# Graph attention layer with routed experts on one core: the last 29 additions of the edge loop in two halves of 132 columns, and the softmax steps of the last chunk in other slots

## What is computed

```
x = x + gnn(layernorm(x), edge_index, edge_attr)
  q = x@Wq+bq; k = x@Wk+bk; v = x@Wv+bv; e = edge_attr@We
  alpha = einsum(q[dst], k[src] + e) / sqrt(32)        # per edge and head
  ea    = exp(alpha - segment_max(alpha, dst)[dst])
  out   = segment_sum((v[src]+e) * ea/denom[dst], dst) + x@Ws+bs
x = x + ffn(layernorm(x))                               # top 2 of 8 experts, 256 -> 512 -> 256
```

## Time and profile before

| what | value |
|---|---|
| median of 3 runs | 2534.5 us (2531.59 to 2537.31) |
| profiled execution, its own time | 2541.5 us |
| span of its trace | 2539.7 us |
| edge loop, last score (L1047) starts | 1944.42 us |
| first addition of the drain starts, last one ends | 1945.44 and 1973.77 us |
| busy over the span: PE, DVE, ACT, POOL | 94, 80, 63, 72% |

### The profile page before, as it was taken

How to read it: one execution, slowest core, us unless ns; L and a number is a source line. 1 busy time by engine, 2 the same in 40 slices (tenths; PEclk the granted TensorE clock), 3 DMA queues, 4 the chain that set the end, 5 groups by cost and what they waited for, 6 DMA issues and landing times. The chain is left out here.

```text
span 2539.7 us, 67202 instructions
## 1 busy us (share of the span) xinstructions
PE 2381.0 (94%) x13310; PEld 1992.7 (78%) x13311; DVE 2021.1 (80%) x5247; ACT 1603.5 (63%) x4423; POOL 1829.9 (72%) x2194
## 2 busy tenths in 40 slices
PE   6998999999999999999999999999998657999998
PEld 3445788888888888888888888888886647999998
DVE  6865999999999999999999999999998863222222
ACT  1222677777677677767767777776776535666665
POOL 4213788888888888888888888887887704666666
PEclk9999999999999999999999999999999558999999
DMA  7325787777777777777777877777777652434443
GB/s 233 130 107 183 235 227 223 225 228 228 219 226 228 222 226 228 222 219 226 227 219 225 230 222 226 226 227 213 228 224 215 196 157 50 71 63 64 69 66 53
DMA packets 337646, 476.68 MB, mean 188 GB/s; under 512 B 61270, under 2 KB 268444, under 8 KB 337004
## 3 DMA queue, kind: packets, MB, share of 16 engines
q0 software_dynamic: 92576, 259.72, 38.2%
q1 hardware_dynamic: 238444, 213.23, 28.6%
q10 hardware_dynamic: 6288, 0.05, 0.1%
HBM read 425.40 MB, written 50.57 MB: 187 GB/s over the span
## 5 line engine op out<-in xcount | busy, mean ns | idle before, releaser
L824 POOL DMA_INDIRECT kv_ring<-vk_table,tab_c x880 | 860.1, 977 | 287.8 <-issue 179.9
L978 PE MATMUL ps_e<-we_sb,aT 128*128 128x256 f32 x3520 | 919.8, 384 | 29.7 <-DVE ve_ke L1065 24.3
L978 PEld LDWEIGHTS ps_e<-we_sb,aT 128*128 128x128 f32 x3520 | 600.9, 191 | 105.5 <-issue 51.3
L1059 DVE TENSOR_TENSOR ve_ke<-kv_ring,ps_e 128x512 f32<-128x512 f32 x880 | 601.0, 683 | 37.9 <-PE ps_e L982 16.2
L834 POOL TENSOR_TENSOR ve_ke<-ve_ke 128x256 f32<-128x256 f32 x880 | 552.7, 632 | 18.8 <-ACT factor L951 5.2
L1029 PE MATMUL ps_u<-ve_ke,sel 128*128 128x264 f32 x1760 | 545.6, 392 | 21.2 <-POOL ve_ke L834 7.0
L911 ACT COPY aT<-ps_t 128x256 f32<-128x256 f32 x880 | 325.8, 370 | 308.2 <-PE ps_t L966 278.0
L982 PE MATMUL ps_e<-q_slots,selT 128*128 x1760 | 517.8, 375 | 0.0
L1129 DVE SCALAR_TENSOR_TENSOR node_slots<-node_slots,same_tile,ps_u 128x264 f32 x880 | 423.9, 482 | 28.2 <-PE ps_u L1029 21.2
L982 PEld LDWEIGHTS ps_e<-q_slots,selT 128*128 128x128 f32 x1760 | 335.2, 190 | 45.9
L1047 DVE TENSOR_REDUCE alpha<-ve_ke 128x8 f32<-128x256 f32 x880 | 366.4, 416 | 5.4 <-issue 3.4
(11 more groups left out here) (251 smaller groups left out, 2687.9 us busy)
## 6 DMA issues: line engine op xcount, KB each, us to landing
a_ring<-in_edge_attr SPq DMA_DIRECT2D x880, 128.0 KB
loc_c<-loc_table SPq DMA_DIRECT2D x220, 128.0 KB
kv_ring<-vk_table,tab_c POOLq DMA_INDIRECT x880
vk_table<-kv_out SPq DMA_DIRECT2D x49, 256.0 KB, 2.0
skip_table<-skip_out SPq DMA_DIRECT2D x49, 128.0 KB, 1.7
out<-node_slots SPq DMA_DIRECT2D x1, 6144.0 KB
node_slots<-skip_table SPq DMA_DIRECT2D x2, 2688.0 KB, 16.8
w_sb<-in_L_ffn_W SPq DMA_DIRECT2D x2, 2048.0 KB, 9.5
```

The costliest lines, as they stand in the source:

```text
L824: g.indirect_dma_start(out=kv_ring[:, i % N_KV, :], out_offset=None, in_=vk_table, in_offset=bass.IndirectOffsetOnAxis(ap=tab_c[:, c % N_T ...
L978: t.matmul(ps_e[i % 2][:, 0:D], aT[i % 2][:, k * P:(k + 1) * P], we_sb[:, k, :], start=(k == 0), stop=(k == KD - 1))
L1059: v.tensor_tensor(ve_ke[:, to:ke + 1:ke - to, 0:D], kv.rearrange("p (t d) -> p t d", t=2), e[:, None, :].to_broadcast([P, 2, D]), ALU.add) ...
```

## The change

Three things are changed, all after the last score.

- In `emit(NCH, ...)` and `emit(NCH + 1, ...)`, that is for all 29 additions of the drain, VectorE adds columns 0 to 131 and columns 132 to 263 in an instruction each. The first half waits for a new semaphore `first_half_added` of the item before (the first of all for `acc_added`), the second half for `acc_added`, which only second halves count.
- The softmax parts of the last chunk stand in other slots: VectorE 2, 3, 4, 5, 6 instead of 3, 4, 6, 7, 8; TensorE 0, 2, 4, 6 instead of 0, 3, 6, 10; ScalarE 1, 2, 6 instead of 3, 4, 11.
- GpSimd applies the mask of the last chunk in slot 11 instead of 5, so behind eleven weighed items (its products) instead of five.

```diff
-            s, at, grant = counters(c3, a_turned=N_A, aT_ready=2, e_ready=2, ve_added=N_KV, kq_ready=2,
+            s, at, grant = counters(c3, a_turned=N_A, aT_ready=2, e_ready=2, ve_added=N_KV, first_half_added=0, kq_ready=2,
...
-            def over_chunks(eng, emit, **kw):
+            def over_chunks(eng, emit, last_parts={}, **kw):
...
-                emit(NCH, NCH % 2, plan(scores=False, **kw))
+                emit(NCH, NCH % 2, plan(scores=False, **dict(kw, parts=last_parts)))
...
-                over_chunks(pool, emit, what="weigh", parts={5: "mask"})
+                over_chunks(pool, emit, what="weigh", parts={5: "mask"}, last_parts={11: "mask"})
...
-                over_chunks(act, emit, what="select", parts={3: "apart", 4: "offs", 11: "exp"})
+                over_chunks(act, emit, what="select", parts={3: "apart", 4: "offs", 11: "exp"},
+                            last_parts={1: "apart", 2: "offs", 6: "exp"})
...
-                over_chunks(pe, emit, what="sum", parts={0: "keys", 3: "scores", 6: "minima", 10: "turn_scores"})
+                over_chunks(pe, emit, what="sum", parts={0: "keys", 3: "scores", 6: "minima", 10: "turn_scores"},
+                            last_parts={0: "keys", 2: "scores", 4: "minima", 6: "turn_scores"})
...
-                def add(c, i, n, before):
+                IN_HALVES_FROM = (NCH - 2) * CH + CH - LAG["add"]
+
+                def add(c, i, n, before, in_halves):
                     m = c * CH + i
                     to, sofar = [sums_flat[:, bass.ds(k * SLOT, UW)] for k in (n, before)]
                     dve.wait_ge(s["summed"], at("summed", m))
+                    if in_halves:
+                        split = m - IN_HALVES_FROM
+                        half = UW // 2
+                        if split:
+                            dve.wait_ge(s["first_half_added"], split)
+                        else:
+                            dve.wait_ge(s["acc_added"], at("acc_added", m - 1))
+                        v.scalar_tensor_tensor(out=to[:, 0:half], in0=sofar[:, 0:half], scalar=same_tile[:, m:m + 1], in1=ps_u[i % 2][:, 0:half],
+                                               op0=ALU.mult, op1=ALU.add).then_inc(s["first_half_added"], 1)
+                        dve.wait_ge(s["acc_added"], at("acc_added", m - 1))
+                        v.scalar_tensor_tensor(out=to[:, half:UW], in0=sofar[:, half:UW], scalar=same_tile[:, m:m + 1], in1=ps_u[i % 2][:, half:UW],
+                                               op0=ALU.mult, op1=ALU.add).then_inc(s["acc_added"], 1)
+                        return
...
-                            add(c - back, i, n, before)
+                            add(c - back, i, n, before, c >= NCH)
...
-                over_chunks(dve, emit, what="add", parts={3: "scan", 4: "scan_back", 6: "own", 7: "least", 8: "shift"})
+                over_chunks(dve, emit, what="add", parts={3: "scan", 4: "scan_back", 6: "own", 7: "least", 8: "shift"},
+                            last_parts={2: "scan", 3: "scan_back", 4: "own", 5: "least", 6: "shift"})
```

## The result

The changed kernel takes 2544.5 us, the median of 6 runs (2542.83 to 2548.24), against 2533.2 us for the kernel before in the same rounds (2531.39 to 2537.31): a ratio of 1.0045, 95% interval 1.0032 to 1.0058, so 8.1 to 14.7 us slower. The forecast was 2539.2 in a range of 2532 to 2545. The direction was right, and the time lies half a microsecond inside the upper end of the range, but the cost is 11.3 us by the medians, 2.4 times the 4.7 us of the sum.

What follows compares the result with a forecast made beforehand. The prediction took VectorE's sequencer work per addition to bound the drain. Halves 3.9, last item 0.1 and softmax steps 0.7 sum to +4.7 us on 2534.5, giving 2539.2 us, range 2532 to 2545.

Steps and rivals of the forecast that it cites:

- VectorE's sequencer is the bound: Drain additions: the sequencer's work per item sets their distance, which goes from 0.83 to 0.97 us, +3.9 us; chance 0.70.
- The third case: Drain additions: data are the bound, 0.69 us per item with halves, -3.1 us in all, 2531.4 us; chance 0.10.
- the second (the sequencer waits for the engine): Drain: next load only once the engine has taken the second half, 0.27 us per item, 2542.9 us; chance 0.10.
- The load behind least: Drain, item 8: by a skill rule this table load would run ahead, item 8 and the sum 0.6 us less.
- The fourth case: Drain: TensorE, granted half its clock throughout, becomes the bound at 1.06 us per item, 2541.7 us; chance 0.10.
- The softmax steps: Drain, items 3 to 15: stalls of 3.5 us against 2.8 with the new slots, +0.7 us, bounds -0.3 and +1.3.
- The hole behind least: Drain, items 8 to 9: the sum of item 9 waits behind turn_scores, so its addition comes 1.88 us after item 8.
- The mask costs nothing: GpSimd, last chunk: the mask waits for the last alpha until 1945.02 anyway and no drain sum needs a product; 0 us.
- nothing outside these 28 us is changed: Whole kernel: the change touches only the drain of 28.33 us, from first to last halved addition; no cost elsewhere.
- Everything up to 1945 as before: Sign expected in the new profile: all rows ahead of the drain's additions unchanged, 0 us.
- what the drain gains or loses should pass to the end one for one: Drain's end: later stages start from a barrier after the last addition, so all +4.7 us reach the total.
- worth nothing, and nothing waits for it later: ScalarE's exponential in the drain: about 1.5 us earlier, but its weights are first needed after 1958; gain 0.

## Why the prediction was right, and where it was not

**Right: VectorE's sequencer is the bound, and each item gets 0.14 us dearer.** The distance went from 0.83 to 0.97 in every kernel with halves. Without the table load and its register work it fell to 0.68 and 0.74. The third case (the data) wanted 0.69 with the loads in place, the second (the sequencer waits for the engine) 1.10; both are out. The load behind least did not run ahead of it: least starts at 1951.11, the load at 1951.1, and item 8 comes 1.74 us behind item 7, as forecast (1.72).

**The fourth case, TensorE at half its clock, came in part.** It was priced for the whole drain. For TensorE alone (us, busy, granted clock, DMA share, GB/s), four stretches of the drain of the changed kernel:

```profile
1944.20:1948.30 4.10, 3.98 (x11) 0.50 1.09 371
1952.60:1958.90 6.30, 6.07 (x13) 0.50 0.98 318
1959.10:1965.80 6.70, 3.60 (x11) 1.00 0.00 1
1966.10:1969.00 2.90, 2.90 (x6) 0.50 0.00 0
```

Between and behind the three stretches at 0.50 the clock is at or near 1.00. By the mean clocks of the drain, 0.79 and 0.94, some 14 us of 34.89 run at the 1.2 GHz level, against some 3.5 of 28.33 in before (an estimate). Two of the additions of the last such stretch, VectorE in order of time:

```profile
1967.25 0.35 DVE L1139 SCALAR_TENSOR_TENSOR node_slots<-node_slots,same_tile,ps_u 128x132 f32 x1 [0.55 <-PE ps_u L1030]
...
1969.37 0.35 DVE L1139 SCALAR_TENSOR_TENSOR node_slots<-node_slots,same_tile,ps_u 128x132 f32 x1 [0.54 <-PE ps_u L1030]
```

The additions ahead start at 1966.09 and 1968.22, so 1.16 and 1.15 us earlier instead of 0.97, and TensorE ends the wait. The distances are 1.16, 0.97, 1.15 and 0.97 in turn, 1.06 in the mean, just the chain that the prediction gave for half the clock. Behind item 9 there are two more of 1.15 and 1.14. The four together cost 0.7 us. Why the clock falls where it does stays open: it fell behind pauses of TensorE of 3.44, 2.39 and 1.65 us here, and did not fall in before behind one of 1.93 (ahead of the sum at 1961.47).

**The softmax steps: right in kind, small in size.** The hole behind least was forecast at 1.88 us, the first halves show 1951.94 to 1954.31, 2.37. TensorE and VectorE in order of time, which answer to the earlier trace rows:

```profile
1952.47 0.28 DVE L1103 TENSOR_TENSOR least<-ps_ak,least 128x128 f32<-128x128 f32 x1
1954.31 0.35 DVE L1139 SCALAR_TENSOR_TENSOR node_slots<-node_slots,same_tile,ps_u 128x132 f32 x1 [1.56 <-PE ps_u L1030]
...
1952.81 0.47 PE L1024 MATMUL ps_rx<-ident,least 128*128 128x128 f32 x1 [2.39 <-DVE least L1103]
1953.08 6.21 PE L1030 MATMUL ps_u<-ve_ke,sel 128*128 128x264 f32 x12
```

The mechanism is the one described: turn_scores waits for shift, and the sum of item 9 stands behind it. But transpose and sum ran slow there, at a granted clock of 0.50 behind 2.39 us of idle TensorE: the upper bound of that term. Item 3 to item 15 takes 16.66 us in the changed kernel, 15.91 with the mask put back, 15.16 in the forecast; the rescaling in the drain takes 2.33 and 2.51 instead of 2.76, and the fifteen distances behind it 15.3 and 15.2 instead of 14.6, in the changed kernel by the two distances at half clock above and one pause of 0.35 us (below).

**Wrong: "The mask costs nothing."** This is the step that failed. It looked at what waits for a product or the mask and found nobody, which is true: with the factor in PSUM nothing ahead of T0 is late. What it did not look at is what GpSimd's products do to VectorE while they run. The prediction had eleven products back to back from 1937.55 to 1944.4, and the rescaling stood right in that stretch. This is also where "nothing outside these 28 us is changed" and the sentence on the change, "all after the last score", went wrong: the mask's slot is behind the last score in the program, but GpSimd's row of products starts 10.30 us ahead of T0 in time. "Everything up to 1945 as before" was the sign that would have shown it, and it did not hold. The row cost 3.41 us ahead of T0 and 0.5 to 0.7 behind it. The second part goes with TensorE's clock. For the 4 us from T0 (for TensorE alone: us, busy, granted clock, DMA share, GB/s), the kernel with only the mask moved:

```profile
1940.03:1944.03 4.00, 3.11 (x9) 0.50 1.07 374
```

and the one with the mask moved and the factor in PSUM:

```profile
1929.86:1933.86 4.00, 2.83 (x9) 1.00 0.82 219
```

In the first, TensorE had stood still for 3.45 us behind the late rescaling and then ran at the 1.2 GHz level until 6.4 us behind T0; the first scan starts 3.61 us behind T0 instead of 3.10 in before, and GpSimd's last row 12.55 instead of 12.07. In the second it stayed at 2.4 GHz. (The same four us show 0.83 in before, where the clock falls 2.6 us behind T0, and 1.00 in the two kernels with halves and the mask behind five products.) But the late rescaling is not the whole of it: with the factor in PSUM the later mask costs 0.51 us behind T0 all the same. The first nine us are nearly alike there, then the clock falls 9.8 us behind T0 instead of 10.3, just at turn_scores, and GpSimd's last row starts 12.08 us behind T0 instead of 11.58. So the half microsecond follows where the half clock falls on the chain to the exponential. Whether the mask's slot puts it there, or chance does, no run shows.

One rule of the Trainium skill describes this conflict (SBUF — State Buffer, Who interferes with whom): a VectorE instruction with two inputs in SBUF contends with a GpSimd instruction that reads SBUF, and one with at most one input there does not. The traces agree on both, 3.95 us against 0.41. The same page of the Trainium skill (SBUF: two separate sides) says that whoever starts first has the shared ports for its whole instruction and the other blocks. That would be one product of some 0.59 us; here VectorE was kept out for 3.95 - 0.53 = 3.4 us, nearly six of them. The measured number decides what such a conflict costs: in this place, nearly the whole rest of GpSimd's row.

**Wrong: "what the drain gains or loses should pass to the end one for one."** In before the additions did not set the end of the stage; GpSimd's drain did, by 1.14 us. Where the last product leads, `den` starts 9.64 us behind its end: 1965.89 and 1975.53 in before, 1957.15 and 1966.79 without loads, 1954.28 and 1963.92 with the new slots as well. So "worth nothing, and nothing waits for it later", said of the exponential, was wrong as well: GpSimd's last row of products waits for what ScalarE writes there (L951, 5.21 us of idle time in before) and sets the end of the stage in before. The chain of the earlier trace rows was followed to its last addition but not to the first instruction of the next stage, where 1.76 us of idle time would have shown it.

**Two errors that hid each other.** The 4.73 us of the kernel with the mask put back are just the sum that was forecast, and this is partly luck. Its additions end 5.87 us later after T0, not 4.7, and 1.14 of that is what GpSimd's drain had cost anyhow. Halves alone gave +4.06 and slots alone +0.65 at `den` (forecast 4.0 and 0.7), but each with 1.14 taken off: at the end of the additions they are +5.20 and +1.79. What the forecast lacked is by the rows the hole behind least and the longer distances, both at half clock, and the two pauses of 0.35 us.

The sum as it should have read: 5.9 for halves and slots at the end of the additions, less the 1.1 that GpSimd's drain had cost anyhow, 3.4 for the rescaling behind GpSimd's row, 0.7 behind T0, 8.8 us.

## What to carry to other kernels

Before an engine's instructions are put in a longer unbroken row, look at what the other engines read and write during that row, not only at who waits for its results. Here it was VectorE's operation with two SBUF operands while GpSimd multiplied, and moving one small operand to PSUM took some 8 us off the kernel. A step that stands behind a point in the program can start work ahead of it in time. Follow the end of a stage to the first instruction of the next one; an idle time there can belong to an engine whose last work ended long ago by its rows. And where a sequencer's work per instruction is the bound, splitting an instruction adds to it however short the halves are: 0.14 us for each of the 29 here.

## What the runs showed of the hardware that was not expected

- A VectorE operation with two SBUF operands was kept waiting by GpSimd's products until half a microsecond before the end of their row: 0.53, 2.22 and 3.95 us for rows of five, eight and eleven. Over all 55 chunks of the kernel before, in most of which GpSimd's products stand singly between DMA issues, it takes 418 to 784 ns, 582 in the mean, against 412 to 420 with one operand in PSUM.
- It does not always happen. The rescaling of the last chunk falls inside the row of sixteen products (1954.02 to 1963.42 in the changed kernel), starts at 1961.79 and lasts 0.58 us; over all kernels with the factor in SBUF it lasts 0.42 to 0.90 there. Why VectorE got in there and not in the row of eleven stays open.
- GpSimd's drain instruction takes 15.9 to 16.1 us and ends 9.0 to 9.1 us after its last product by the rows, in all kernels. What it does in these 9 us no run shows.
- In every kernel with halves and table loads two distances are 1.32 or 1.33 instead of 0.97 us, at the same items: that from 13 to 14 and that from 12L to 13L. At the second TensorE has its full clock. The sequencer's rows of the changed kernel show it at work there: its register work starts at 1975.7, and the SEQ_ASSERT, which otherwise follows 0.2 to 0.3 us later, at 1976.3. The cause of these pauses of 0.35 us stays open.
